# Gated graph layers and graph attention on one core: the row of neighbour terms goes through DRAM instead of through PE transposes

## What is computed

```python
def _L0_gnn_ref(x, adj, weight, w_ih, w_hh, b_ih, b_hh):
    A = (adj != 0).astype(x.dtype)
    h = x
    for i in range(3):
        m = einsum('bnd,de->bne', h, weight[i])
        aggr = einsum('bst,bsd->btd', A, m)
        h = _gru_cell(aggr, h, w_ih, w_hh, b_ih, b_hh)
    return h

def _L1_gnn_ref(x, adj, W, a):
    h = einsum('bsf,of->bso', x, W)
    f_i = h @ a[0, :128]
    f_j = h @ a[0, 128:]
    e = f_i[:, :, None] + f_j[:, None, :]
    e = where(e >= 0, e, 0.2 * e)
    att = softmax(where(adj > 0, e, NEG), axis=2)
    return einsum('bij,bjo->bio', att, h)

h = maximum(_layernorm(x), 0);  x = x + _L0_gnn_ref(h, adj, ...)
h = maximum(_layernorm(x), 0);  x = x + _L1_gnn_ref(h, adj, ...)
```

## Time and profile before

| | |
|---|---|
| median of 3 runs | 479.29 us (477.17 to 480.46) |
| profiled execution, its own time | 480.37 us |
| span of the profile | 477.4 us, 8140 instructions |
| PE busy | 456.3 us (96%) |
| DVE busy | 426.7 us (89%) |
| ACT busy | 355.5 us (74%) |
| POOL busy | 141.7 us (30%) |
| chain that ended last, by engine | PE 87%, DVE 6%, ACT 4% |
| DMA | 26.41 MB, mean 55 GB/s |

### The profile page before, as it was taken

The page is one execution under the profiler, slowest core; times in us unless marked ns, Lnnn a source line. Parts: engine busy times, 40 slices in busy tenths (PEclk is TensorE's granted clock), DMA queues, the critical chain, the costliest instruction groups (busy, mean ns, idle before and its releaser), DMA issues.

```text
span 477.4 us, 8140 instructions
## 1 busy us (share of the span) xinstructions
PE 456.3 (96%) x2584; PEld 385.0 (81%) x2584; DVE 426.7 (89%) x1085; ACT 355.5 (74%) x640; POOL 141.7 (30%) x169
## 2 busy tenths in 40 slices
PE   8799999999999999999999999999999999989586
PEld 7577787788888888888888888888888888867485
DVE  4878998999999999999999999999999998987743
ACT  3457667778978797878978797878978797867364
POOL 3122453242324223241424124232423223223200
PEclk9989999999999999999999999999999999998859
DMA  8400020201202030201202030200203000000001
GB/s 327 175 1 0 9 103 2 110 2 51 84 23 110 24 110 24 86 26 37 97 23 111 22 112 22 91 23 24 109 22 112 22 2 24 0 24 0 24 1 45
DMA packets 7242, 26.41 MB, mean 55 GB/s; under 512 B 800, under 2 KB 800, under 8 KB 5152
## 3 DMA queue, kind: packets, MB, share of 16 engines
q1 hardware_dynamic: 7200, 25.90, 14.9%
HBM read 21.70 MB, written 4.19 MB: 54 GB/s over the span
## 4 chain that ended last, share of the span: by engine, by line
PE 87%; DVE 6%; ACT 4%; issue 2%; POOL 1%; DMA 1%; DVEq 0%; SPq 0%
PE X L1181 18%; PE G L1297 12%; PE G L1286 6%; PE R L1165 5%; PE R L1166 4%; PE R L1167 4%; PE Z L1167 4%; PE Z L1165 4%; PE Z L1166 4%; PE X L1231 3%; PE G L1264 2%; PE HN L1165 2%; PE HN L1167 2%; PE HN L1166 2%; PE IN L1167 2%; PE IN L1165 2%
## 5 line engine op out<-in xcount | busy, mean ns | idle before, releaser
L1181 PE MATMUL X<-A_ring,nat_hi 128*128 128x512 f32 x192 | 79.3, 413 | 1.0 <-DVE nat_lo L747 1.0
L1181 PE MATMUL X<-A_ring,nat_lo 128*128 128x512 f32 x192 | 76.1, 397 | 0.0
L1297 PE MATMUL G<-hp,probT 128*128 128x128 f32 x512 | 67.0, 280 | 0.7 <-DVE out_sb L864 0.7
L1297 PEld LDWEIGHTS G<-hp,probT 128*128 128x128 f32 x512 | 64.0, 196 | 2.2 <-issue 0.9
L852 DVE SCALAR_TENSOR_TENSOR prob<-e 128x512 f32<-128x512 f32 x64 | 49.1, 767 | 12.4 <-ACT e L444 11.1
L382 ACT CAST agg_hi<-X 128x512 fp32r<-128x512 f32 x48 | 28.2, 587 | 35.9 <-PE X L1181 35.8
L262 POOL TENSOR_TENSOR hT_lo<-hT,hT_hi 128x512 fp32r<-128x512 f32 x19 | 24.5, 1290 | 92.1 <-ACT hT_hi L370 72.3
L402 ACT ACTIVATE tr<-R,bias 128x512 f32<-128x512 f32 x48 | 33.4, 695 | 24.6 <-PE R L1167 24.6
L443 ACT ACTIVATE e<-g,nb 128x512 f32<-128x512 f32 x64 | 46.4, 724 | 6.7 <-DVE nb L845 6.7
L1181 PEld LDWEIGHTS X<-A_ring,nat_hi 128*128 128x128 f32 x192 | 36.7, 191 | 11.2 <-DVE nat_lo L747 3.1
L444 ACT ACTIVATE e<-g,nb 128x512 f32<-128x512 f32 x64 | 45.7, 714 | 0.0
(11 more groups left out here) (125 smaller groups left out, 1201.6 us busy)
## 6 DMA issues: line engine op xcount, KB each, us to landing
adj_raw<-in_adj SPq DMA_DIRECT2D x16, 1024.0 KB, 4.9
x_ring<-in_x SPq DMA_DIRECT2D x16, 256.0 KB, 2.7
out_x<-out_sb SPq DMA_DIRECT2D x16, 256.0 KB, 2.0
inner_in<-in_inner SPq DMA_DIRECT2D x1, 384.0 KB, 6.1
outer_in<-in_outer SPq DMA_DIRECT2D x1, 325.0 KB, 5.5
```

The costliest lines, as they stand in the source:

```text
L1181: mm = pe.matmul(X[:], part[s][:, c], A_ring[:, (k - s) % RING, c], start=(c == 0 and part is nat_hi), stop=(c == C - 1 and part is nat_lo))
L1297: mm = pe.matmul(G2[:, c * D:(c + 1) * D], probT[:, c % 2, j], hp[:, (k + 1) % 2, j, 0:D], start=(j == 0), stop=(j == C - 1))
```

## The change

The neighbour terms no longer pass PE. SP stores column D+1 of hp, 128 partitions with 4 words each, to a DRAM tensor `row` of 512 words in node order, waits until it has landed, and loads those 2 KB into each of the 128 partitions of a new SBUF tile fj. `scores` waits for that load and reads fj instead of G0. `neighbour_terms` is gone from PE, and turn_result no longer waits for the scores. In the code of SP, the new step stands between the loads and the store of a pass. The order of calls on PE, DVE, ACT and POOL was written anew, in the prologue, in `full` and in the end; `full` also begins at another place of the pass.

```diff
+        fj = sb("fj", [P, N])
+        row = nc.dram_tensor("row", (C, P), F32, kind="Internal").ap()
...
+            def neighbour_row(i, k):
+
+                if on(i, GB):
+                    sp.wait_ge(hp_done, i - (GB - 1))
+                    if on(i - 1, GB):
+                        sp.wait_ge(row_loaded, (i - GB) * 16)
+                    sp.dma_start(row.rearrange("c p -> p c"), hp[:, (k + 1) % 2, :, D + 1],
+                                 allow_slow_non_contiguous=True).then_inc(row_stored, 16)
+                    sp.wait_ge(row_stored, (i - (GB - 1)) * 16)
+                    if on(i - 1, GB):
+                        sp.wait_ge(g_done, (i - GB) * C)
+                    sp.dma_start(fj[:], row.rearrange("c p -> (c p)").partition_broadcast(P)).then_inc(row_loaded, 16)
...
             for i in range(1, ITERATIONS + 1):
                 if on(i, 0):
                     load_x(i, i % RING)
                     load_adjacency(i, i % RING)
+                neighbour_row(i, i % RING)
                 if on(i, GB + 1):
                     store(i - (GB + 1))
...
             def scores(i, k):
 
                 if on(i, GB):
-                    dve.wait_ge(fj_mm, i - (GB - 1))
+                    dve.wait_ge(row_loaded, (i - (GB - 1)) * 16)
                     for c in range(C):
-                        dve.tensor_tensor_reduce(out=g[:, k % 2, c], in0=G0[:], in1=neg_ring[:, k, c], scale=1.0,
+                        dve.tensor_tensor_reduce(out=g[:, k % 2, c], in0=fj[:], in1=neg_ring[:, k, c], scale=1.0,
...
                 if on(i, GA):
                     pe.wait_ge(h_done, through(i - 1, 2))
-                    if on(i, GB) and not gru_done(i):
-                        pe.wait_ge(g_done, (i - (GB - 1)) * C)
...
-            def neighbour_terms(i, k):
-
-                if on(i, GB):
-                    pe.wait_ge(hp_done, i - (GB - 1))
-                    for c in range(C):
-                        mm = pe.transpose(G0[:, c * P:(c + 1) * P], hp[:, (k + 1) % 2, c, D + 1:D + 2].broadcast_to([P, P]), ident[:])
-                    mm.then_inc(fj_mm, 1)
...
             def full(i):
...
+                from_neighbours(i - 1, (i - 1) % RING, 0, R)
+                project(i - 1, (i - 1) % RING)
+                turn_state(i - 1, (i - 1) % RING, 2)
+                from_state(i - 1, (i - 1) % RING, 0, Z)
+                from_neighbours(i - 1, (i - 1) % RING, 0, IN)
                 from_neighbours(i - 1, (i - 1) % RING, 0, Z)
-                project(i - 1, (i - 1) % RING)
                 neighbours(i, i % RING, 2)
                 from_state(i, i % RING, 2, Z)
-                neighbour_terms(i, i % RING)
```

More of the change, by code:

```diff
@@ L867, in full @@
             def full(i):
+                x_mean(i, i % RING)
+                mask(i - 1, (i - 1) % RING)
+                natural_low(i - 1, (i - 1) % RING, 2)
+                reset(i - 1, (i - 1) % RING, 0)
                 before_tanh(i - 1, (i - 1) % RING, 0)
+                state_low(i - 1, (i - 1) % RING, 2)
                 keep(i - 1, (i - 1) % RING, 0)
-                state_low(i - 1, (i - 1) % RING, 2)
                 renew(i - 1, (i - 1) % RING, 0)
@@ L1301, in full @@
             def full(i):
+                from_neighbours(i - 1, (i - 1) % RING, 1, IN)
+                turn_prob(i - 1, (i - 1) % RING, 2)
+                neighbours(i - 1, (i - 1) % RING, 0)
+                turn_prob(i - 1, (i - 1) % RING, 3)
+                attend(i - 1, (i - 1) % RING, 2)
+                attend(i - 1, (i - 1) % RING, 3)
+                from_state(i - 1, (i - 1) % RING, 0, HN)
+                turn_normed(i - 1, (i - 1) % RING)
+                from_state(i - 1, (i - 1) % RING, 0, R)
@@ L1315, in full @@
                 from_state(i, i % RING, 1, R)
+                from_state(i, i % RING, 1, Z)
+                turn_prob(i, i % RING, 0)
+                from_neighbours(i, i % RING, 1, Z)
                 from_state(i, i % RING, 1, HN)
-                turn_prob(i, i % RING, 0)
-                from_state(i, i % RING, 1, Z)
+                turn_prob(i, i % RING, 1)
+                from_neighbours(i, i % RING, 1, R)
                 turn_input(i, i % RING)
-                from_neighbours(i, i % RING, 1, Z)
@@ L1332, in full @@
-                turn_normed(i, i % RING)
-                attend(i, i % RING, 2)
-                attend(i, i % RING, 3)
-                from_neighbours(i, i % RING, 0, R)
-                turn_state(i, i % RING, 2)
-                from_state(i, i % RING, 0, Z)
             busy()
+            turn_input(0, 0)
+            make_wi(2)
+            make_wi(0)
             make_wa()
-            turn_input(0, 0)
-            make_wi(0)
-            make_wi(1)
             neighbours(0, 0, 0)
-            make_wi(2)
+            from_state(0, 0, 0, R)
@@ L1411, in _ @@
             neighbours(3, 3, 0)
+            project(3, 3)
             from_state(3, 3, 0, R)
-            turn_normed(3, 3)
+            from_neighbours(3, 3, 0, R)
             from_state(3, 3, 0, HN)
-            from_neighbours(3, 3, 0, R)
+            turn_state(3, 3, 2)
             from_state(3, 3, 0, Z)
-            project(3, 3)
-            turn_state(3, 3, 2)
             from_neighbours(3, 3, 0, IN)
```

498 lines of the change are left out of this document (241 added, 257 removed).

## The result

| | before | after |
|---|---|---|
| median of the runs | 478.62 us (477.17 to 480.46) | 641.69 us (641.02 to 644.62) |
| ratio | | 1.341 (1.336 to 1.347) |
| span of the profile | 477.4 us | 639.2 us |
| PE busy, share of the span | 96% | 75% |
| chain that ended last, by engine | PE 87%, DVE 6%, ACT 4% | DMA 35%, PE 32%, ACT 8%, DVE 8% |

The account below looks back on a forecast made before the run. PE, without gaps at 27.0 us a graph, was taken as the bound. Transposes -4.8, pass 4 -1.4 and the end +0.5 gave -5.7 us: 474.7 in the profile's terms, 473.6 in the median's, range 471 to 484.

Parts of the forecast that it names:

- The store of row: SP's DMA of 512 separate 4-byte words to DRAM: lands in 2.0 us, bounds 1.3 and 4.2.
- rival 3: The stored words are dear: at 4.2 us the row lands 1.7 us after it is wanted, 495 us in all; chance 0.15.
- The load: SP's second DMA, writing 128 rows of 2 KB as x_ring's does: lands in 2.7 us.
- When the row is wanted: First score on DVE at about x = 3.6; row landed at 3.06, 0.5 us early, bounds 2.4 and 5.3.
- x: Time in us within a pass, counted from the start of PE's step-2 neighbour sum, x = 0.
- Late row, one for one: Lateness beyond about 0.65 us makes PE wait equally long, once in each of 12 passes.
- The transposes: Removing PE's groups of four saves 0.44 us each, 11 in passes with full PE: 4.8 us.
- rival 2: New order stalls elsewhere with the row in time: 0.1 to 0.3 us a pass, 475 to 482 us; chance 0.12.
- The score steps read SBUF instead of PSUM, so 0.: DVE's score steps take 0.68 us, as do a step reading PSUM and one reading SBUF alone: cost 0.
- Moved steps: 0: Same steps on the same engines in another order cost 0, up to 0.3 us per pass (3 us) for the range.
- Pass 4 and the start: Pass i = 4 gains 0.44 + 0.98, about 1.4 us; the start, to 82 us, 0, plus or minus 1.
- The end: Last graphs, where the row's 4.76 us are not covered: +0.5 us, from 0 to +4.

Follow-up runs that it names:

- one_transpose: The kernel before with only the first of the four neighbour-term transposes in each pass; 478.26 us, ratio 0.998.
- old_order_short_pool: The kernel before without the four transposes, fj from a DRAM row filled once, POOL's hT_lo step cut to 32 of 512 columns from graph 5; 477.99 us.
- no_store: The changed kernel without the store of the row; fj is loaded from a DRAM row filled once at the start; 490.27 us, ratio 1.024.
- new_order_pe: The changed kernel's order of calls without the DMAs, four transposes back on PE, graph 17's end partly as before; 482.94 us, ratio 1.009.
- no_store_short_pool: no_store with POOL's hT_lo step cut to 32 of 512 columns from graph 5 on; 481.73 us, ratio 1.006.

## Why the prediction was wrong, step by step

- **The store of row.** Taken as 2.0 us, bounds 1.3 and 4.2; it was 9.0. This is the step that failed. Both ends were worked out from rows of 2 KB pieces, the upper one as a price per piece. The price doesn't go by the number of pieces but by where they land: 512 words apart from each other took 1.8 us. That the 2.0 meets this is luck, since its reason (four times the pieces against 1/512 of the bytes each) never looked at the place. The sign was rival 3's, but its 495 us was far off too: a bound per piece can't hold a cost that comes from neighbours.
- **The load.** Taken as 2.7; 5.0 behind such a store, 3.3 behind none. The sum had no term for a load that reads what was just stored word by word (1.7 us); 0.6 over x_ring's was a small error.
- **When the row is wanted.** x = 3.6; DVE was free at 3.88. hp at x = -1.70; it was -1.78. The geometry of the new order was right to 0.3 us.
- **Late row, one for one.** Right for PE's wait (8.27 us late, 8.19 us of wait). The lower clock behind each gap, about 2.0 us a pass, was missing: the sum has no term for what a PE does after a long wait.
- **The transposes.** 0.44 us a group was the right price of PE's work and the wrong one of the kernel's time. "PE has no gap" was read as "PE alone bounds": one_transpose and old_order_short_pool show 27.01 and 27.06 us a pass, where the price gives 26.7 and 26.6. The prediction had noticed 0.05 to 0.2 us of room before turn_state (for hT) and named it under rival 2, but subtracted the full 4.8 us nonetheless. In the new order the same holds in part: 26.95 with the transposes, 26.83 without them and without the wait for POOL, 0.12 of the 0.44.
- **"The score steps read SBUF instead of PSUM, so 0."** Wrong. The rows compared were a step from PSUM and one from SBUF, each alone; none beside a POOL step. It costs 12 us in the old order. In the new order no score step stands beside POOL's, and it costs nothing there (0.691 us in no_store).
- **"Moved steps: 0", up to 0.3 us a pass.** Too small: 0.77 us a pass in no_store (27.60, and 26.83 with POOL's step cut), 8.5 us in all. The rooms were looked for between PE and DVE; what cost was nb beside POOL's step, two steps that share no tile and no semaphore.
- **Pass 4 and the start.** Pass 4, taken as 1.4 us shorter, was not: from step-2 sum to step-2 sum 28.12 us before, 28.29 in new_order_pe, 28.85 in no_store. In new_order_pe the wait for nat_lo is gone there, as said, but one of 0.60 for prob stands in its place; in no_store the first row is 3.1 us late and PE waits 0.92 for nat_lo again. The start, taken as 0, plus or minus 1, gave 1.2: by so much new_order_pe's step-2 sum of pass 3 is ahead (57.83 and 59.06).
- **The end.** Taken as +0.5, bounds 0 to +4. The order alone costs 5.1 us there (new_order_pe). A row that comes in 3.3 us adds nothing to that: from the last issue of adj_raw to the end no_store has 122.3 us and new_order_pe 122.5. The prediction priced the row in the end and took the order of the rest as free.

Even with a row in time the forecast would have been wrong by 17 us (no_store 490.3). The runs split no_store's +11.6 us over the kernel before into +4.2 for the new order with its end (new_order_pe), -1.2 for the transposes (from there to no_store_short_pool, within the spread of the two runs) and +8.5 for nb beside POOL (from there to no_store); the three come from differences of the same runs, so that their sum is no test. Of the changed kernel itself this part is not shown: there nb is not stretched (0.162 us on average), so the 0.4 us by which its pass without the row's wait is above 27.0 stay open. None of the kernels tried is faster than the one before by what a measurement can tell.

## What to carry to other kernels

Before a small row goes through DRAM, look at where its pieces land: single words side by side are the dear case, and a row of before with wider pieces can't bound it. When an operand moves from PSUM to SBUF, or steps move in time, list the steps of GpSimd that run beside each VectorE step that reads SBUF twice: here two such steps shifted by 0.17 us against each other are what a kernel that pays 8.5 us has and its neighbour hasn't. And before work taken off a full engine is counted as time, find the instruction behind it that waits for another engine with less room than the gain: here DVE's agg_lo, which left none.

## What the runs showed of the hardware

- 512 stores of 4 bytes side by side in DRAM land 9.0 us after issue (8.2 where the load behind reads another row), 128 of them 7.3 us; 16, 32, 64 and 512 bytes apart, 512 of them land in 2.6, 1.9, 1.8 and 1.8 us; 128 pieces of 16 bytes side by side in 1.4 us.
- A load of 128 times the same 2 KB takes 5.0 us right behind a store of its row word by word, 3.1 to 3.3 us from another row or one that was not just written, 3.8 us behind the store of whole pieces, and 5.0 to 5.1 us without any store where it was issued 0.4 us behind a load of 1 MB.
- A DVE step of 512 numbers with both inputs in SBUF, 0.16 us alone or when it started 0.09 us ahead of POOL's, took 1.23 when it started 0.08 us behind; a score step 1.77 and not 0.68, and POOL's 1.61 and not 1.29. A score step with one input in PSUM took 0.69 beside the same POOL step.
- After 8.2 us without work PE had a mean granted clock of 0.52 for 4.4 us; ten matmuls took 4.33 us in it and not 2.3.
